# Up biases carried as a weight row, weights less their first row by gathers that add, and an earlier last mixing table

## The reference, cut to what matters

```python
xn = layernorm(x)                       # x: (2, 2048, 256), no scale and no shift after the norm
# attention branch: v and r from xn, a recurrence over time with decay and first, then out_w
# expert branch, for every token t (4096 tokens, 8 experts, the best 2 by softmax):
h = silu(xt @ w1e.T + b1e) * (xt @ w3e.T + b3e)        # 256 -> 256 and 256 -> 256
y = h @ w2e.T + b2e                                    # 256 -> 256
# shared branch: the same form with 512 hidden columns
out = x + attention(xn) + gate_1 * y_1 + gate_2 * y_2 + shared(xn)
```

## Time and profile before

| | us |
|---|---|
| median of 3 runs | 533.35 (531.29 to 537.48) |
| the profiled execution | 534.84 |
| its span, first to last instruction | 533.1 |
| PE busy | 466.8 (88%) |
| DVE busy | 404.6 (76%) |
| POOL busy | 237.3 (45%) |
| ACT busy | 215.2 (40%) |
| mean granted TensorE clock, share of full | 0.933 |

### The profile page before, as it was taken

The page is one execution under the profiler, slowest core; times in us unless marked ns, Lnnn a source line. Parts: engine busy times, 40 slices in busy tenths (PEclk is TensorE's granted clock), DMA queues, the critical chain, the costliest instruction groups (busy, mean ns, idle before and its releaser), DMA issues. The chain is left out here.

```text
span 533.1 us, 8639 instructions
## 1 busy us (share of the span) xinstructions
PE 466.8 (88%) x2624; PEld 386.5 (73%) x2624; DVE 404.6 (76%) x736; ACT 215.2 (40%) x361; POOL 237.3 (45%) x208
## 2 busy tenths in 40 slices
PE   1786084899999999999999929699999999999997
PEld 1332042688888888888888817598889888888887
DVE  7796997277787876878776607899888878787964
ACT  1676252154554365555554523314232414232321
POOL 2000002645182836547464248885646472737100
PEclk9998555799999999999999968799999999999999
DMA  7999200326542443433354338325262534344011
GB/s 229 390 363 341 103 0 20 100 80 204 152 142 90 144 141 112 139 101 128 110 141 146 100 114 311 114 80 201 64 195 69 188 91 165 107 150 134 25 41 39
DMA packets 44310, 74.13 MB, mean 139 GB/s; under 512 B 5904, under 2 KB 32272, under 8 KB 44272
## 3 DMA queue, kind: packets, MB, share of 16 engines
q1 hardware_dynamic: 37792, 55.94, 29.9%
q0 software_dynamic: 6480, 17.70, 12.3%
HBM read 45.39 MB, written 28.18 MB: 138 GB/s over the span
## 5 line engine op out<-in xcount | busy, mean ns | idle before, releaser
L843 POOL DMA_INDIRECT xg<-xn_rows,tile_tok x71 | 70.2, 988 | 116.7 <-POOLq L313 84.2
L1288 POOL DMA_INDIRECT yg<-expert_rows,rows x64 | 70.7, 1104 | 23.4 <-issue 17.1
L899 PE MATMUL ps_g<-w_hi,x_hi 128*128 x142 | 56.8, 400 | 0.4 <-issue 0.4
L1319 PE MATMUL ps_w<-col_hi,s_hi 128*128 128x512 f32 x128 | 51.9, 405 | 5.9 <-DVE shid L1526 4.1
L899 PE MATMUL ps_g<-w_lo,x_hi 128*128 x142 | 56.8, 400 | 0.0
L899 PE MATMUL ps_g<-w_hi,x_lo 128*128 x142 | 56.6, 399 | 0.0
L1041 DVE SCALAR_TENSOR_TENSOR act<-act,ps_g 128x512 f32<-128x512 f32 (+1 forms) x36 | 24.0, 668 | 42.3 <-ACT act L966 37.4
L1320 PE MATMUL ps_w<-col_lo,s_hi 128*128 128x512 f32 x128 | 51.2, 400 | 0.0
L1321 PE MATMUL ps_w<-col_hi,s_lo 128*128 128x512 f32 x128 | 51.1, 400 | 0.0
L1421 ACT ACTIVATE sact<-ps_w,vec_b 128x512 f32<-128x512 f32 x32 | 22.0, 688 | 60.8 <-PE ps_w L1321 44.5
L1526 DVE SCALAR_TENSOR_TENSOR shid<-ps_w,vec_b,sact 128x512 f32<-128x512 f32 x32 | 24.0, 749 | 28.5 <-ACT sact L1421 16.1
(11 more groups left out here) (198 smaller groups left out, 1321.7 us busy)
## 6 DMA issues: line engine op xcount, KB each, us to landing
expert_rows<-y SPq DMA_DIRECT2D x35, 256.0 KB
table<-mix_tables SPq DMA_DIRECT2D x8, 768.0 KB, 5.2
xin<-x SPq DMA_DIRECT2D x16, 256.0 KB, 4.6
xn_rows<-xn SPq DMA_DIRECT2D x16, 256.0 KB, 4.6
xn_columns<-xT SPq DMA_DIRECT2D x8, 512.0 KB, 4.7
col<-xn_columns SPq DMA_DIRECT2D x8, 512.0 KB, 3.9
res<-x SPq DMA_DIRECT2D x16, 256.0 KB
out<-res SPq DMA_DIRECT2D x16, 256.0 KB
```

Of the source, the lines that this page charges most:

```text
L843: pool.indirect_dma_start(out=xg[b][:, t, :], out_offset=None, in_=xn_d[:, :], in_offset=bass.IndirectOffsetOnAxis(ap=tile_tok[:, 2 * a + ...
L899: nc.tensor.matmul(out, x[:, k, :], w[:, ds(e, 1), k, cols].rearrange("p o n -> p (o n)"), start=(k == 0 and n == 0), stop=False)
L1288: pool.indirect_dma_start(out=yg[a.buf(2)][:, k, q, :], out_offset=None, in_=y_d[:, :], in_offset=bass.IndirectOffsetOnAxis(ap=picked[a.bu ...
L1319: nc.tensor.matmul(out, w_hi, x_hi, start=start, stop=False)
```

## The change

1. A new input `w_first` holds row 0 of each expert's two up matrices (8 x 512). The 256 contraction rows of the up part are now rows 1 to 255 and, as the last one, the up bias. The rows of `xn` get a 257th element that is always 1; what is stored to `xn_rows` for the gathers is elements 1 to 256. The columns that the gate and the mix use stay as they were.
2. Since x_0 = -(x_1 + ... + x_255), weights less their row 0 give the same product. The subtraction is done by DMA: POOL negates `w_first` (L426 of the new file), stores it with eight zero rows as `first_rows` in DRAM (L428), and after each weight piece has landed issues an indirect transfer with addition (L437) that adds row e of `first_rows` to the 512 up columns in all 128 partitions of the piece. For half k = 1 the index of partition 127, the bias row, points at a zero row (`row_of1`). ACT's `split` waits for this transfer (`s_less`) and no longer for the load (`s_w`).
3. `up` has no bias matmul any more; `down` keeps its own. `bias_hl` shrinks from 768 to 256 columns.
4. End of run_experts: the last reciprocal (`invert(v - 1, 3)` of the last piece), `factors` of the last piece and its store stand one pair earlier, `vr_hi` and `vr_lo` too; the block no longer waits for the last table's store. The mix waits for it in its second step (`coef_stored`).

```diff
     xn_d = nc.dram_tensor("xn_rows", (TOK, C), F32, kind="Internal").ap()
     xT_d = nc.dram_tensor("xn_columns", (P, NSTEP, KC * STEP), F32, kind="Internal").ap()
     tab_d = nc.dram_tensor("mix_tables", (T // PIECE, P, 3, KC, PIECE), F32, kind="Internal").ap()
+    nw_d = nc.dram_tensor("first_rows", (2 * E, 2 * FF), F32, kind="Internal").ap()
...
+        coef_stored = kept.enter_context(nc.semaphore("coef_stored"))
...
+            firsts1 = sb("firsts1", [P, 2, KC, PIECE], F32, experts, "right")
...
-            bias_hl = sb("bias_hl", [P, E, WALL], F32R, experts, "right")
+            bias_hl = sb("bias_hl", [P, E, C], F32R, experts, "right")
...
-        xn = [sb(f"xn{b}", [P, Q, C], F32) for b in range(2)]
+        xn = [sb(f"xn{b}", [P, Q, C + 1], F32) for b in range(2)]
...
+        w_neg = sb("w_neg", [2 * E, 2 * FF], F32)
+        off127 = sb("off127", [P, 1], F32)
+        row_of1 = sb("row_of1", [P, E], I32)
+        BR = E * C // P
...
                 for i in range(1, NX):
                     load_x(At(0, i, NSTEP))
+                    if i == 1:
+                        sp.wait_ge(s_negz, 1)
+                        sp.dma_start(w_neg[0:E, :], w_first).then_inc(s_negl, 16)
                 for i in range(SOON):
                     load_w(i)
...
-                                     xn[a.buf(2)][:, b * HALF:(b + 1) * HALF, :]
+                                     xn[a.buf(2)][:, b * HALF:(b + 1) * HALF, 1:C + 1]
...
+                nc.gpsimd.memset(w_neg[:], 0.0).then_inc(s_negz, 1)
...
                 nc.gpsimd.memset(pick2[0:2, :], 1.0).then_inc(s_two, 1)
 
+                pool.wait_ge(s_negl, 16)
+                nc.gpsimd.tensor_scalar(w_neg[:], w_neg[:], -1.0, None, ALU.mult).then_inc(s_neg, 1)
+                pool.wait_ge(s_neg, 1)
+                pool.dma_start(nw_d, w_neg[:]).then_inc(s_negd, 16)
+
+                pool.wait_ge(s_negd, 16)
+                pool.wait_ge(s_row1, 1)
+                for i in range(E * KC):
+                    e, k = divmod(i, KC)
+                    index = lane_i[:, e:e + 1] if k == 0 else row_of1[:, e:e + 1]
+                    pool.wait_ge(s_w[i % NW], (i // NW + 1) * 16)
+                    pool.sem_inc(s_lgo, 1)
+                    pool.indirect_dma_start(
+                        out=w_raw[i % NW][:, 0:2 * FF], out_offset=None, in_=nw_d,
+                        in_offset=bass.IndirectOffsetOnAxis(ap=index, axis=0), compute_op=ALU.add
+                    ).then_inc(s_less[i % NW], 16)
...
-                    nc.scalar.activation(bias_hl[:, a.i, :].bitcast(F32), ident[:, 0:1].broadcast_to([P, WALL]),
+                    nc.scalar.activation(bias_hl[:, a.i, :].bitcast(F32), ident[:, 0:1].broadcast_to([P, C]),
...
 
                 def split(i):
-                    act.wait_ge(s_w[i % NW], (i // NW + 1) * 16)
+                    act.wait_ge(s_less[i % NW], (i // NW + 1) * 16)
                     nc.scalar.activation(w_parts[0][:, i, :], w_raw[i % NW], ACT.Copy).then_inc(s_whi, 1)
...
-                nc.vector.tensor_copy(lane[:], lane_i[:])
+                nc.vector.tensor_copy(lane[:], lane_i[:]).then_inc(s_lane, 1)
                 nc.vector.tensor_copy(lane_b[:], lane_i[:, :, None].broadcast_to([P, P, BATCH]))
                 nc.vector.tensor_copy(base_b[:], base_i[:])
-                nc.vector.tensor_copy(row[:], row_i[:])
+                nc.vector.tensor_copy(row[:], row_i[:]).then_inc(s_lane, 1)
                 nc.vector.tensor_copy(desc[:], desc_i[:])
+                dve.wait_ge(s_lane, 2)
+                nc.vector.tensor_scalar(off127[:], row[:], float(P - 1), float(E), ALU.is_ge, ALU.mult
+                                        ).then_inc(s_off, 1)
+                dve.wait_ge(s_off, 1)
+                nc.vector.tensor_scalar(row_of1[:], lane[:, 0:E], off127[:], None, ALU.add).then_inc(s_row1, 1)
                 nc.vector.tensor_copy(ones[:], ones_f[:])
+                for b in range(2):
+                    nc.vector.memset(xn[b][:, :, C:C + 1], 1.0)
                 dve.wait_ge(s_two, 2)
                 nc.vector.tensor_copy(ones2[:], pick2[:])
                 nc.vector.memset(keep[:], 1.0)
@@ -567,7 +610,7 @@
...
-                  sb("firsts", [P, 2, KC, PIECE], F32)[:]]
+                  firsts1[:]]
...
-                    if r == 3 and 0 < v <= NPIECE:
+                    if r == (2 if v == NPIECE else 3) and 0 < v <= NPIECE:
...
-                sp.wait_ge(t_cst, NPIECE * 16)
...
+                def cut(n, parts):
+                    raw, hi, lo = parts
+                    pool.wait_ge(c_whi, n + 1)
+                    nc.gpsimd.tensor_tensor(lo[:], raw[:], hi[:].bitcast(F32), ALU.subtract).then_inc(c_wlo, 1)
...
-                    if r == 2 and 0 < v <= NPIECE:
+                    if r == 1 and v == NPIECE:
+                        cut(0, vr)
+                    if r == (1 if v == NPIECE else 2) and 0 < v <= NPIECE:
                         factors(v - 1)
                     if r == 3 and v < NPIECE:
                         denominator(v)
-                for n, (raw, hi, lo) in enumerate((vr, col)):
-                    pool.wait_ge(c_whi, n + 1)
-                    nc.gpsimd.tensor_tensor(lo[:], raw[:], hi[:].bitcast(F32), ALU.subtract).then_inc(c_wlo, 1)
+                cut(1, col)
 
...
-                def three(out, hi, lo, e, cols):
+                def three(out, hi, lo, e, cols, last):
                     for k in range(KC):
                         for n, (x, w) in enumerate([(hi, w_hi), (hi, w_lo), (lo, w_hi)]):
-                            nc.tensor.matmul(out, x[:, k, :],
-                                             w[:, ds(e, 1), k, cols].rearrange("p o n -> p (o n)"),
-                                             start=(k == 0 and n == 0), stop=False)
-                    return nc.tensor.matmul(out, ones2[:],
-                                            bias_hl[:, ds(e, 1), cols].rearrange("p o n -> p (o n)"),
-                                            start=False, stop=True)
+                            mm = nc.tensor.matmul(out, x[:, k, :],
+                                                  w[:, ds(e, 1), k, cols].rearrange("p o n -> p (o n)"),
+                                                  start=(k == 0 and n == 0), stop=(last and k == KC - 1 and n == 2))
+                    return mm
...
                     for t in range(tiles(a)):
                         mm = three(ps_g[a % 2][:, t, :], x_hi[a % 2][:, t], x_lo[a % 2][:, t], es[t],
-                                   slice(0, 2 * FF))
+                                   slice(0, 2 * FF), True)
...
-                        mm = three(ps_y[a % 2][:, t, :], h_hi[a % 2][:, t], h_lo[a % 2][:, t], es[t],
-                                   slice(2 * FF, WALL))
+                        three(ps_y[a % 2][:, t, :], h_hi[a % 2][:, t], h_lo[a % 2][:, t], es[t],
+                              slice(2 * FF, WALL), False)
+                        mm = nc.tensor.matmul(ps_y[a % 2][:, t, :], ones2[:],
+                                              bias_hl[:, ds(es[t], 1), :].rearrange("p o n -> p (o n)"),
+                                              start=False, stop=True)
...
-                    if a == DUOS - 3:
+                    if a == DUOS - 4:
                         act.wait_ge(c_vr, 16)
...
                         if 0 < v <= NPIECE:
                             invert(v - 1, 2)
+                        if v == NPIECE:
+                            invert(v - 1, 3)
                     if r == 2:
                         if v < NPIECE:
                             scan_b(v)
-                        if 0 < v <= NPIECE:
+                        if 0 < v < NPIECE:
                             invert(v - 1, 3)
...
                 def step(a, first, left):
+                    if isinstance(a.i, int) and a.i == 1:
+                        sp.wait_ge(coef_stored, NPIECE * 16)
...
+    up = np.concatenate([cols("L0_ffn_w1"), cols("L0_ffn_w3")], axis=2)
+    bias = np.concatenate([get("L0_ffn_b1"), get("L0_ffn_b3")], axis=1)
...
-        "w_all": np.concatenate([cols("L0_ffn_w1"), cols("L0_ffn_w3"), cols("L0_ffn_w2")], axis=2),
-        "b_all": np.concatenate([get("L0_ffn_b1"), get("L0_ffn_b3"), get("L0_ffn_b2")], axis=1).reshape(-1),
+        "w_all": np.concatenate([np.concatenate([up[:, 1:], bias[:, None]], axis=1), cols("L0_ffn_w2")], axis=2),
+        "w_first": up[:, 0],
+        "b_all": get("L0_ffn_b2").reshape(-1),
```

More of the change, by code:

```diff
@@ L178, in build, with route @@
                         wvr.rearrange("(k p) n -> p k n", p=P), xT_d[:, 0, :])
-        mix(nc, x, xT_d, y_d, y_stored, tab_d, out, slots, gates, vr_hi, vr_lo, raw_s13, raw_o, raw_s2,
+        mix(nc, x, xT_d, y_d, y_stored, coef_stored, tab_d, out, slots, gates, vr_hi, vr_lo, raw_s13, raw_o, raw_s2,
             col0, col_hi0, col_lo0, vec_b1, vec_b3, row_b2)
-def route(nc, x, first, decay, vec_tf, vec_td, gate_w, gate_b, w_all, b_all, xn_d, xT_d, ident, slots, gates,
```

(3 more changed lines are left out.)

29 lines of the change are left out of this document (18 added, 11 removed).

## The result

The changed kernel took 528.78 us in the median against 535.54 for the kernel before (20 runs each); the ratio is 0.9882, with a 95% interval from 0.9855 to 0.9909. So it is faster by 1.2%, or 6.3 us (4.9 to 7.8) of 535.5, where 16.6 were forecast; none of the 20 times is as low as 517.

A forecast was written before the change was run, and what follows sets the result against it. PE's matmuls were taken to bound the experts, DMA and DVE the route, a barrier the experts' end. −16.5 + 1.0 − 3.8 + 0.7 − 0.5 + 2.5 = −16.6 from 534.84, less 1.5 for the median: 517 us, range 509 to 531.

The forecast's parts named there:

- Experts, what is removed: Experts stage: 71 up bias matmuls go, at 0.2325 us each, −16.5 us; a pair of tiles would take 5.34 us.
- Experts, what is late next: Experts, four to five late waits of ACT: each gives back half of a pair's gain, 0.23 us; +1.0 us.
- rival B: Experts: the chain of late waits sets the pace, its period staying at 23.57 us; 11 us lost, 528 us; chance 0.14.
- End of the experts: Barrier before mix: POOL's tail moves with its last operation, 312.7 against 316.5 us; −3.8 us, bounds 0 and −9.4.
- Route, small items: Route: added casts, index operations and fills on DVE, +0.7 us; shorter bias fills on ACT, −0.5 us.
- The −0.5 in it: Route, ACT: eight bias_hl fills of 256 instead of 768 columns save 0.5 us each, little on the path; −0.5 in all.
- Route, the gathers with addition: Route: sixteen 256 KB transfers cost +2.5 us in the step loop (bounds 0 and 8), 0 behind it.
- the second place: Route, gathers of pieces 8 to 15 from about 51 us: hidden while one takes up to 3.1 us, 2.3 taken; 0.
- Rival C: Route: slow gathers hold ACT's splits of pieces 8 to 15, making the kernel slower than before; chance 0.16.
- G: Time in us per adding gather in the route; at 5.2 us the other gains of 16.6 us are eaten.

The follow-up runs named there:

- e11: Kernel before, with POOL's gathers seven pairs ahead instead of six, on the third chip: 532.24 us, ratio 0.9979.
- e10: Changed kernel, with POOL's gathers seven pairs ahead instead of six, on the third chip: 521.56 us, ratio 0.9773.
- e9: Changed kernel as it is, run again on the third chip: 528.39 us, ratio 0.9872 to the kernel before.
- e13: Changed kernel once more, one execution on the third chip: 524.90 us, the kernel before 538.33.
- e15: Kernel before with only the reordered end of the experts, one execution on the third chip: 533.71 us, the kernel before 538.33.
- e6: Kernel before with only the reordered end of the experts, on the second chip: 530.74 us, ratio 0.9982.
- e7: Changed kernel, with POOL subtracting the first row, spread by plain transfers, instead of the adding gathers, on the second chip: 526.30 us, ratio 0.9939.
- e12: Changed kernel with gathers seven pairs ahead and 26 unread matmuls behind PE's last one of the experts, third chip: 518.63 us, ratio 0.9695.
- e3: Changed kernel without the route's sixteen adding gathers, so the first row is not subtracted: 521.76 us, ratio 0.9726.
- e4: Changed kernel with the route's sixteen gathers copying over the weights instead of adding: 523.96 us, ratio 0.9787.
- e1: Changed kernel with the experts' gathers replaced by plain transfers of other rows: 516.64 us, ratio 0.9673.

## Why the prediction was wrong

**Experts, what is removed (−16.5): right in kind, 1.6 us too much.** A pair takes 5.35 us, 5.34 was forecast. With no late signals in either, from the first up matmul to PE's last one of the experts is 207.4 us in e11 and 192.5 in e10: −14.9. I had multiplied by a distance of starts rounded up; 5.79 − 5.35 is 0.22 for each matmul, not 0.2325, and the last pairs give less.

**Experts, what is late next (+1.0): the step that failed.** The rows were there, with the 0.14 us of cover and a period of 23.57 us, but I took the late result for a wait that gives back only half of what one pair gains, 0.23 us at each of four to five places. It is set by a ring that PE is in only by its held signals, and that does not get shorter when PE does: DVE's last inversion, POOL's factors, two gathers, three operations for the denominators, six gathers in a row, the release of PE's signals 1.2 to 1.3 us behind them, ACT's `act`, and DVE's work up to the next last inversion. In the changed kernel these are 192.69 → 198.39 (ACT, DVE), → 200.94 (factors), → 206.84 (two gathers, denominators), → 214.35 (six gathers), → 215.62: 22.9 us, against 21.4 of PE. It cost 8.0 us (200.5 against 192.5 in e10) instead of 1.0; against e10 on its own chip, e9 and e13 lose 6.7 and 7.5. In the kernel before PE's 23.2 us hid it but for 0.7 (2.4 in e15 against e6, the same code on two chips). This is rival B, at 0.14, by another price, 22.9 in place of 23.57, and by a mechanism that nothing in the prediction has: that PE's signals are held. Without it the changed kernel's pairs take the 5.35 us that were forecast, as in e7 with the same runs of six.

**End of the experts (−3.8): right.** −3.7, and the tail of 5.9 us behind POOL's last operation stayed as long; all kernels with the new order but e12, which fills the gap, show 6.92 to 6.95 us between the last matmul and mix. The tail moved with POOL's last operation, and neither stayed where it was (0) nor shrank (−9.4).

**Route, small items (+0.2): right in the sum,** 0.3 in e3. The −0.5 in it does not follow from its rows: 0.06 us between 568 and 768 columns makes 0.15 us for each fill, not 0.5.

**Route, the gathers with addition (+2.5): mis-sized, +6.7 in e3.** This is the second term that failed, and three steps of it were wrong. I counted eight of the gathers before 42 us; POOL issued four by then (16.39 to 23.6), the fifth at 42.61 and the sixth at 47.98. I let half of 5.2 us vanish in headroom of the loop (365 against 404 GB/s); none did: five gathers are 1.3 MB, 3.2 us at 404 GB/s, and DVE came out of the loop 6.9 us later (`red` at 49.25 instead of 42.35; without the gathers, in e3, it is 43.58). DVE's waits for the rows of xn were 7.8 us in all where 5 to 6 were forecast, and between 28 and 40 us DVE fell to half its load. And I priced an addition as a copy: by e3 and e4 copies cost 4.3 us, additions 6.7. By the sentence from the Trainium skill on two source reads (Collectives: The Full Stack, The bandwidth ceiling) it would have been 5.2; that page's factor of 2 is 1.5 to 1.7 here, by the first gathers of e1 to e4 and the changed kernel. For the second place, the gathers behind the loads, 3.1 us each was the limit and 1.8 measured (1.53 and 0.30 to the next). ACT waited for them 11.6 us in all, so not shortly as the prediction had it, but nearly all in the air that it had: `hot_tok` began at 75.19, 8.3 us late, of which the loop is 6.5 (ACT's table load behind it, 42.22 → 48.69) and this 1.8, and most of that was made up by the end of the route. Rival C did not come: G is a third of its 5.2 us.

**What the sum did not have (−3.0):** the clock in mix. The trace before is one of the six with the late clock, the longer wait for DVE at 338 us and the second fall; the one after is not. Both kinds occur with and without the change (212.2 us of mix in e11, 217.5 in e9), so this seems to belong to the executions rather than to the change, and the ratio of all times has less of it: 6.3 against 7.6 us.

With the measured terms: −14.9 + 7.3 (8.0 less the 0.7 of before) + 6.7 − 3.7 = −4.6, and −3.0 of mix is −7.6, the distance of the two traces; the terms were taken from these traces in part, so that this sum closes is no test of them.

## What to carry to other kernels

When the bounding engine is made faster, look for every period in its trace that is nearly as long as its own work, and follow it round through engines that seem idle: here a cover of 0.14 us, and a ring of 22.9 us where PE wanted 21.4, took back half of the gain, and one constant in the order of the gathers gave it back. Where a stretch is held by transfers at a share of 1.0, count added bytes in full, and an adding transfer as more than one copy (1.5 to 1.7 here). Where times of one kernel fall into groups, compare traces of both groups stage by stage before a difference of two traces is put down to a change. A fix measured on one chip, on which the fault does not occur, shows nothing: run the faulty kernel beside it.

## What was not expected of the hardware

PE's semaphore updates can arrive up to 3.7 us behind the work that they report (188.97 to 192.69) while POOL issues six gathers in a row (1.25 us each), and are released together, 1.2 to 1.5 us behind the run's end. It was in every trace of a kernel with runs of six in the experts, nine of them, but for the two on the second chip; behind runs of two no update was late. It goes away with plain transfers (e1) or with pauses between pairs (e10). What holds them was not found.

An adding gather of 256 KB takes POOL 1.53 us to issue, a copying one 0.94 (e4).
